# Flamingo block on one core: second normalisation through logarithm and exponential, rows on GpSimd, first shared products between the last projections

## The reference, cut to what matters

```python
def _layernorm(x, eps=1e-05):
    return (x - mean(x)) / sqrt(var(x) + eps)

x = x + tanh(g_xattn) * (softmax(q @ k.T * 16**-0.5) @ v @ W_proj + b_proj)   # q from _layernorm(x), k and v from ctx
n = _layernorm(x)                                # the second normalisation
topw, topi = softmax/top_k(n @ gate_w.T, 2)      # the router
shared = silu(n @ sg_gate.T) * (n @ sg_up.T) @ sg_down.T
x = x + tanh(g_ffn) * (shared + sum over the 2 chosen experts e of w_e * (silu(n @ wg[e].T) * (n @ wu[e].T)) @ w_down[e].T)
```

## Time and profile before

| | us |
|---|---|
| median of 3 runs | 488.83 (488.44 to 489.25) |
| the profiled execution, device time | 488.55 |
| its span in the trace | 486.5 |
| outside the span | 2.05 |
| PE busy | 474.4 (98% of the span) |
| DVE busy | 305.7 (63%) |
| ACT busy | 260.9 (54%) |
| POOL busy | 183.9 (38%) |

### The profile page before, as it was taken

The page is one execution under the profiler, slowest core; times in us unless marked ns, Lnnn a source line. Parts: engine busy times, 40 slices in busy tenths (PEclk is TensorE's granted clock), DMA queues, the critical chain, the costliest instruction groups (busy, mean ns, idle before and its releaser), DMA issues.

```text
span 486.5 us, 7717 instructions
## 1 busy us (share of the span) xinstructions
PE 474.4 (98%) x2765; PEld 283.5 (58%) x2765; DVE 305.7 (63%) x575; ACT 260.9 (54%) x416; POOL 183.9 (38%) x216
## 2 busy tenths in 40 slices
PE   8999999999999999999989999999999999999995
PEld 6655523332333233324445465689799899799994
DVE  3776779999999999997465689632333333323332
ACT  2675277777777777776644501305445346344440
POOL 2830178872321111111000014513556747758433
PEclk9999999999999999999999999999999999999998
DMA  8733408766763555211105001323334533544324
GB/s 245 245 99 103 141 10 241 221 173 192 199 163 80 161 167 165 66 35 55 34 0 174 0 3 43 97 77 77 55 49 65 84 53 68 75 68 67 44 32 44
DMA packets 36789, 48.30 MB, mean 99 GB/s; under 512 B 6288, under 2 KB 29968, under 8 KB 36752
## 3 DMA queue, kind: packets, MB, share of 16 engines
q1 hardware_dynamic: 22112, 26.43, 19.5%
q0 software_dynamic: 7344, 9.84, 13.1%
q10 hardware_dynamic: 7296, 11.54, 7.4%
HBM read 30.16 MB, written 14.29 MB: 91 GB/s over the span
## 4 chain that ended last, share of the span: by engine, by line
PE 88%; DVE 5%; ACT 3%; DMA 2%; issue 1%; POOL 0%; SPq 0%; POOLq 0%
PE ps L1290 69%; PE ps L1382 13%; PE ps L1663 2%; PE ps L1674 2%; DMA wkv_sb<-in_w_kv 2%; DVE neg_max L935 1%; PE ps L1696 1%; ACT up_region L694 1%; ACT rows L688 1%; DVE dn_region L929 1%; DVE rows L900 1%; ACT ctx_region L768 1%; PE ps L1374 0%; PE ps L1535 0%; PE ps L1544 0%
## 5 line engine op out<-in xcount | busy, mean ns | idle before, releaser
L768 ACT ACTIVATE ctx_region<-ps 128x512 f32<-128x512 f32 x256 | 140.7, 594 | 46.9 <-PE ps L1290 46.9
L935 DVE TENSOR_REDUCE neg_max<-ps 128x2 f32<-128x1024 f32 x128 | 150.8, 1209 | 20.9 <-PE ps L1290 18.9
L1290 PE MATMUL ps<-unit_region 96*128 96x512 bf16 (+1 forms) x512 | 128.3, 380 | 1.2 <-ACT ctx_region L768 0.7
L1290 PEld LDWEIGHTS ps<-unit_region 96*128 96x128 bf16 (+1 forms) x512 | 45.0, 97 | 101.3 <-ACT ctx_region L768 45.2
L1290 PE MATMUL ps<-unit_region,ctx_region 128*128 128x128 f32 (+1 forms) x824 | 97.4, 274 | 0.0
L1290 PEld LDWEIGHTS ps<-unit_region,ctx_region 128*128 128x128 f32 (+1 forms) x824 | 94.3, 188 | 0.7 <-DVE x_sb L1077 0.3
L662 POOL DMA_INDIRECT out<-unit_region x39 | 61.2, 1570 | 54.2 <-DMA out<-unit_region 32.3
L1290 PE MATMUL ps<-dn_region,unit_region 128*128 (+1 forms) x294 | 70.0, 381 | 0.0
L849 ACT COPY ctx_region<-up_region 128x1536 f32 x33 | 48.5, 1472 | 34.9 <-PE ps L1290 26.3
L1247 DVE TENSOR_TENSOR unit_region<-unit_region,ps 128x384 f32<-128x384 f32 x35 | 19.4, 555 | 71.2 <-ACT unit_region L866 60.5
L1290 PEld LDWEIGHTS ps<-dn_region,unit_region 128*128 128x128 f32 x294 | 53.2, 190 | 8.4 <-issue 2.8
(11 more groups left out here) (201 smaller groups left out, 459.4 us busy)
## 6 DMA issues: line engine op xcount, KB each, us to landing
up_region<-in_w_upT ACTq DMA_DIRECT2D x9, 768.0 KB, 4.7
qk_parts<-up_region SPq DMA_DIRECT2D x24, 192.0 KB, 3.0
unit_region<-qk_parts SPq DMA_DIRECT2D x24, 192.0 KB, 3.9
dn_region<-in_w_downT ACTq DMA_DIRECT2D x9, 384.0 KB, 5.3
unit_region<-up_region SPq DMA_DIRECT2D x48, 64.0 KB, 2.6
unit_region<-qk_parts SPq DMA_DIRECT2D x24, 128.0 KB, 4.0
x_rows<-rows SPq DMA_DIRECT2D x4, 512.0 KB, 3.3
out<-x_sb SPq DMA_DIRECT2D x4, 512.0 KB
```

Source lines behind the costliest of these rows:

```text
L768: nc.scalar.activation(probs[:, k % 8, :], bank(SCORE_HOME[u, k]), ACT.Exp).then_inc(exp_done, 1)
L935: nc.vector.tensor_reduce(neg_max[:, s, 2 * p:2 * p + 2], bank(2 * (p % 2), 2), AX.X, ALU.max, negate=True).then_inc(max_done, 1)
L1290: return nc.tensor.matmul(o_, w, m, start=start, stop=stop)
```

## The change

ACT now makes 1/sqrt(variance + eps) itself as exp(-0.5 * ln(variance + eps)), from one table set that also holds the Exp of the scores and is loaded once, after the Tanh. For batches 0 and 1 this happens inside the last unit, after the Exps of steps 1 and 11. POOL makes the normalised rows of batches 0 to 2; DVE keeps batch 3. PE turns the rows of batch 0 after step 7 of the last unit, DVE copies them to SBUF, and the four products of the shared expert's chunk 0 go between the last projections. PE's order behind them is new: `turn_rows(1)`, `turn_rows(2)`, `shared_up(0, 1)`, `turn_rows(3)`, `shared_up(0, 2)` with all `router` calls between its halves, and `turn_logits` last. Some PSUM banks change: batch 0 is turned into banks 0 and 1, batches 1 to 3 all into banks 6 and 7. SP stores the rows of a batch when POOL (or DVE) has made them.

```diff
+TURN_FIRST_ROWS = 7
+RSTD_AT = (1, 11)
...
-            return bank(2 + t % 2 if t < NT - TB else (0, 3, 1, 2)[t % TB])[:, 0:D]
+            return bank(2 + t % 2 if t < NT - TB else (4, 5, 1, 2)[t % TB])[:, 0:D]
...
-            return bank(((4, 5), (6, 7), (6, 7), (2, 5))[b][c])
+            return bank((0 if b == 0 else 6) + c)
...
+            for b in range(B - 1):
+                pool.wait_ge(rstd2_done, b + 1)
+                for t in range(b * TB, (b + 1) * TB):
+                    last = nc.gpsimd.tensor_scalar(rows[:, t, :], x_sb[:, t, :], mean_var[:, t, 0:1], rstd[:, t:t + 1],
+                                                   ALU.subtract, ALU.mult)
+                last.then_inc(early_rows, 1)
...
             nc.scalar.activation(tanh_g[:, :], gates[:, :], ACT.Tanh).then_inc(tanh_done, 1)
+            nc.scalar.preload_act_table_set("natural_log_exp_and_others")
...
+                    if u == UNITS - 1 and k in RSTD_AT:
+                        rstd_of(RSTD_AT.index(k))
+
+            def rstd_of(b):
+                act.wait_ge(var_done, B + b + 1)
+                nc.scalar.activation(std[:, b * TB:(b + 1) * TB], mean_var[:, b * TB:(b + 1) * TB, 1], ACT.Ln,
+                                     bias=eps_sb[:, 0:1]).then_inc(log_done, 1)
+                act.wait_ge(log_done, b + 1)
+                nc.scalar.activation(rstd[:, b * TB:(b + 1) * TB], std[:, b * TB:(b + 1) * TB], ACT.Exp, scale=-0.5
+                                     ).then_inc(rstd2_done, 1)
...
-            for b in range(B - 1):
-                std_of(b, B + b + 1)
-
+            rstd_of(2)
...
-            copy_rowsT(0)
             copy_rowsT(1)
-            std_of(3, B + 4)
             copy_rowsT(2)
+            rstd_of(3)
             copy_rowsT(3)
...
+                    if t == NT - TB - 3:
+                        dve.wait_ge(rowsT_ps, B + 1)
+                        for c in range(DC):
+                            last = nc.vector.tensor_copy(xnT[:, c, 0:T], rowsT_bank(0, c))
+                        last.then_inc(first_rowsT, 1)
...
-            ln_apply(0, B + 1)
-            ln_apply(1, B + 2)
...
             stats2(3)
-            ln_apply(2, B + 3)
-            ln_apply(3, B + 4)
+            dve.wait_ge(rstd2_done, B)
+            ln_rows(range(NT - TB, NT)).then_inc(rows_done, 1)
...
+            def turn_rows(b):
+                if b < B - 1:
+                    pe.wait_ge(early_rows, b + 1)
+                else:
+                    pe.wait_ge(rows_done, B + 1)
+                if b >= 2:
+                    pe.wait_ge(rowsT_sb, B + b - 1)
...
+            def first_shared(half, c):
+                col = half * HALF
+                last = mm(bank(3 * half), w_up[:, E, c, col:col + P], xnT[:, c, 0:T], c == 0, c == DC - 1)
+                if (half, c) == (1, DC - 1):
+                    last.then_inc(sh_up_ps, 1)
...
+                if (i, k) == (1, TURN_FIRST_ROWS):
+                    turn_rows(0)
...
             pe.wait_ge(attn_done, B * DC - 1)
+            pe.wait_ge(first_rowsT, 1)
             project_half(NT - 2, 0)
+            pe.wait_ge(w_ffn_in, 16 * 2 * (E + 1))
+            first_shared(0, 0)
             pv(UNITS - 1, (UNITS - 1) % NG, TB - 1)
             pe.wait_ge(x1_done, NT - TB)
             for t in (NT - TB, NT - TB + 1, NT - 1):
                 project_half(t, 0)
+            first_shared(0, 1)
             for q in range(2):
                 pe.wait_ge(attn_done, B * DC + q)
                 for t in range(NT - TB + 2 * q, NT - TB + 2 * q + 2):
                     project_half(t, 1)
+                first_shared(1, q)
...
-                pe.wait_ge(rowsT_sb, B + max(b, 2) + 1)
+                if b == 0:
+                    pe.wait_ge(rowsT_sb, B + 3)
...
-            turn_rows(0)
             turn_rows(1)
-            pe.wait_ge(w_ffn_in, 16 * 2 * (E + 1))
-            pe.wait_ge(rowsT_sb, B + 1)
-            pe.wait_ge(x1_done, NT - 2)
-            shared_up(0, 0, True)
             turn_rows(2)
-
-            def turn_last_rows():
-                turn_rows(3)
+            pe.wait_ge(x1_done, NT)
+            shared_up(0, 1, True)
+            turn_rows(3)
+
+            def route_all():
                 for b in range(B):
                     router(b)
-            pe.wait_ge(rowsT_sb, B + 2)
-            pe.wait_ge(x1_done, NT)
-            shared_up(0, 1, True, between=turn_last_rows)
+            shared_up(0, 2, True, between=route_all)
             turn_logits()
-            shared_up(0, 2, True)
```

More of the change, by code:

```diff
@@ L341, in build @@
         std_done = sem("std_done")
+        log_done, rstd2_done = sem("log_done"), sem("rstd2_done")
+        early_rows, first_rowsT = sem("early_rows"), sem("first_rowsT")
         rstd_done = sem("rstd_done")
@@ L501, in _ @@
             for b in range(B):
-                sp.wait_ge(rows_done, B + b + 1)
+                if b < B - 1:
+                    sp.wait_ge(early_rows, b + 1)
+                else:
+                    sp.wait_ge(rows_done, B + 1)
                 sp.dma_start(x_rows_by_tile[:, b * TB:(b + 1) * TB, :], rows[:, b * TB:(b + 1) * TB, :]).then_inc(rows_out, 16)
@@ L1499, in _ @@
             pe.wait_ge(small_in, 16 * 3)
+            def turn_rows(b):
+                if b < B - 1:
+                    pe.wait_ge(early_rows, b + 1)
+                else:
+                    pe.wait_ge(rows_done, B + 1)
+                if b >= 2:
+                    pe.wait_ge(rowsT_sb, B + b - 1)
+                for t in range(TB):
+                    for c in range(DC):
+                        last = nc.tensor.transpose(rowsT_bank(b, c)[:, t * P:(t + 1) * P],
+                                                   rows[:, b * TB + t, c * P:(c + 1) * P], ident[:, :])
+                last.then_inc(rowsT_ps, 1)
+            def first_shared(half, c):
[3 more added lines that the diff above has]
+                    last.then_inc(sh_up_ps, 1)
             def project_between(i, k):
@@ L1525, in _ @@
                     project_half(t, 1)
-            def turn_rows(b):
-                pe.wait_ge(rows_done, B + b + 1)
-                if b == 2:
-                    pe.wait_ge(rowsT_sb, B + 2)
-                elif b == 3:
-                    pe.wait_ge(x1_done, NT)
[L1533 to L1537, removed]
+                first_shared(1, q)
             def router(b):
-                pe.wait_ge(rowsT_sb, B + max(b, 2) + 1)
+                if b == 0:
+                    pe.wait_ge(rowsT_sb, B + 3)
                 for c in range(DC):
```

## The result

The changed kernel takes 491.67 us (median of 9 runs, 489.59 to 492.43) against 488.71 (9 runs): ratio 1.0048, 95% interval 1.0036 to 1.0061: slower. By the medians it is 3.0 us; the ratio is closer to that of the means (491.14 against 488.73), which lie 2.4 us apart. The two differ because the nine runs fall into two groups. Four lie at 489.59 to 490.43 with a mean granted clock of 0.999 to 1.0, five at 491.67 to 492.43 with 0.995 or 0.996. The median is the lowest run of the second group: with one run more in the first it would have been 490.43. The profiled execution (492.14, span 490.0) belongs to the second group.

A forecast was written before the change was run, and what follows sets the result against it. PE was taken as the bound, busy throughout 272.2 to 470 us. It is free 1.92 us earlier but waits 2.7 us for DVE's chunk, starting 0.79 later: 488.83 + 0.8 = 489.6 us, range 488.8 to 492.2.

The forecast's parts named there:

- The stall: PE before the shared expert's second batch: idle 2.7 us for DVE's first hidden chunk behind the logits; start 0.79 us later.
- The forecast: Whole kernel: 489.6 us, with the second batch 0.79 us late and the clock holding; chance 0.60.
- rival (a): PE's stall before the second batch drops its clock, costing 2.1 us more: 491.7 us; chance 0.28.
- a fallen clock: Sign against the prediction: PE's clock falls in the idle of 2.6 us behind `turn_logits`.
- The price: Cost of a fallen clock: 18 small matmuls at cold start took 4.2 us against 2.1, so 2.1 lost.
- the bound of 0.2%: About 0.2% (0.98 us) of the kernel's time is what a measurement can tell from no change.
- Part 1: Last attention unit: early transposes 0.93 us, Ln and Exp 0.53, POOL's row operation 0.73; last `pv` starts 250.22 against 249.12.
- Part 2: PE's tail from the last `pv`: 1.3 us idle before `turn_rows(2)`, batch 3 ready 0.3 us early, `turn_logits` done at 270.21.
- Part 3: Tables and queues: the prologue's new table load (1.28 us) costs nothing under ACT's idle; earlier row stores precede gathers by 50 us.
- Rival (b): ACT's Ln and Exp each force a table load, 2 x 1.28 us a pair: 494.3 us; chance 0.05.
- Rival (c): The first hidden chunk does not hold PE up at the second batch, keeping 1.92 us: 486.9 us; chance 0.07.

The follow-up runs named there:

- Experiment 1: Changed kernel with Silus and products of hidden chunks 0 and 1 moved ahead of the logits on ACT and DVE: 487.48 us, ratio 0.9971.
- experiment 3: Kernel before, with only PE's new order: whole third chunk of batch 0, router between its halves, ahead of turning the logits: 492.32 us, ratio 1.0079.
- experiment 2: Changed kernel with 16 filler transposes of the identity on PE behind `turn_logits`, results unused: 490.45 us, ratio 1.0039.
- experiment 6: Changed kernel with DVE's 16 MAX8 done twice more ahead of the first hidden chunk, lengthening PE's stall: 494.97 us, ratio 1.0121.
- experiment 5: Changed kernel with batch 3's rows turned between the second chunk's halves and logits between the third's, after the router: 490.01 us, ratio 1.0019.
- experiment 7: Experiment 1 with batch 2 turned into banks 2 and 5, so PE need not wait for ACT's copy of batch 1: 485.99 us, ratio 0.994.
- 9: Changed kernel with 21 filler transposes of the identity on PE behind `turn_logits`, results unused: 490.5 us, ratio 1.0028.
- experiment 4: Kernel before, with only the logarithm and exponential table set load added behind the Tanh: 488.78 us, ratio 0.9999.
- experiment 10: Experiment 1 with the early products undone: batch 0 turned behind the last projections, its four products in one piece: 488.51 us, ratio 0.9985.

## Why the prediction was right, and where not

**The stall.** Right in place, cause and size. Forecast: `turn_logits` issued 19.99 us after the last `pv` starts, chunk 2.7 us later, second batch 0.79 us late. Measured: 271.00 + 0.44 - 251.28 = 20.16, then 2.71, and the second batch 1.00 late, counted from the start of the last unit. Experiment 1 shows the cause by taking it away, experiment 3 by adding it alone.

**The clock.** This is the step that decided, and I weighted it too low. The forecast (489.6, 0.60) was that the clock holds; rival (a) (491.7, 0.28) that it falls. The prediction gave a fallen clock as a sign that it is wrong, and in the profiled execution it fell. Four of nine runs did the one (their mean is 490.1), five the other (492.0), and the median fell into the second group, at 491.67, where (a) had put it. That it matches (a) to 0.03 us is luck. The price was 2.1 in the forecast, 1.5 us in the trace and 1.9 between the means of the groups, and its source is weak: the 18 small matmuls at the kernel's start, which took 4.2 us, took 3.61 in the changed kernel's trace (1.5 us by the same working), and the profile gives both stretches a granted clock of 1.00, so it does not show that the clock made them slow.

The chance had been read from one fall at the kernel's end, 2.24 us after the last matmul. That row was enough to name the case and too little to weigh it. In the twelve traces the fall at that place comes anywhere from 2.3 to 5.1 us after the last matmul: 2.3 in three of them (the kernel before, experiments 2 and 6), 4.9 or more in four (3, 5, 7 and 9). In the stall of the changed kernel it came after 2.0. A stall of 2.55 us lies at the short end of this spread, so it could go either way, and one of 1.30 lies below all of it. The page's rule (the Trainium skill, TensorE: Matmul & The Clock Gate, "What's actually happening") says that the chip looks at TensorE's activity in windows that run freely, not aligned with the kernel; the two outcomes at one idle length (a fall in the changed kernel's trace, none in experiment 3's) and the spread at the kernel's end agree with that. What I had drawn from it, that a stall shorter than a window never costs anything and the time is 489.6, is not what the stall of 2.55 us did in five of nine runs.

**My direction.** Slower had 0.55 and same 0.36; it was slower, clear of the bound of 0.2%. The single number I gave was on the edge of "same", 2.1 us under the result; the range up to 492.2 held it, because it took in rival (a). Even the group whose clock held lies 0.5 us over the forecast; the changed stretch accounts for 0.2 of that (1.00 in place of 0.79), and the rest is open.

**Part 1.** The last unit went as written: 0.93 us forecast for the eight transposes, 0.88 measured (243.03 to 243.91), Ln and Exp 0.52 against 0.53, the last `pv` 1.14 us later relative to the unit's start (251.28 - 235.16 against 249.12 - 234.14). DVE's two copies took 1.29, inside 0.8 to 1.7. POOL's row operation was mis-sized: 0.73 taken, 1.22 measured, inside the bounds. It cost nothing, since batch 0 was ready at 242.54 and needed at 243.03, but the cover (the time by which the rows were early) shrank from 2.5 us to 0.5. Batch 2's rows were there at 258.58, 1.7 us before use; in experiment 7 only 0.3 are left.

**Part 2.** The idle of 1.3 us ahead of `turn_rows(2)`: 1.25. The rows of batch 3: ready at 264.30, transposes at 264.61, so 0.3 us ahead as forecast.

**Part 3.** The table load cost nothing (experiment 4). The earlier stores of the rows were not tried by themselves; the kernel behind the changed stretch took as long as before. Rival (b) fell: no load at either pair. Rival (c) fell: PE did wait.

**What the change is worth without the stall:** 1.3 us (experiment 1), not the 1.92 that rival (c) would have kept; 0.7 to 1.0 of it is the early turning and the products laid between the projections (experiment 10).

## What to carry to other kernels

A step moved to the end of one engine's stretch also moves everything that stands behind its result in another engine's list: here two independent pieces of work (a hidden chunk, the routing) shared DVE's list in the wrong order, and putting the one that PE needs first turned a loss of 3 us into a gain of 1.3 (3.0 with experiment 7's banks). A stall of TensorE can have a second price beyond its length: here the one of 2.55 us had it in some executions, the one of 4.99 us in all four, and those of 1.30 us and less in none as far as the clocks show. Break it up, fill it, or move the wait, and look at every run's time and at the clock of the stretch in a trace, rather than at the median alone. Before copying such an edit, see whether the engine it loads has idle time there: the same edit in the old order cost 1 us.

## What the runs showed of the hardware that I had not expected

With TensorE idle, the granted clock fell 2.0 us after the last matmul in the changed kernel, 3.8 in experiment 6, and 2.3 to 5.1 at the end of the twelve profiled kernels; in experiment 3's trace it did not fall in 2.55 us at all. In the traces with waits of 0.83 and 1.30 us (experiment 5) and 0.80 (experiment 2) it held, and none of the ten other runs of experiment 5 is above 490.4. With 4.99 us it fell in all 4 runs, by the trace of one and the means of the rest. Once down it stayed for 3.4 us in the changed kernel and for 6.8 in experiment 6.

GpSimd's tensor_scalar with two per-partition operands took 1.22 us for 128x256 floats, where its tensor_tensor of that size took 0.73 and VectorE's tensor_scalar a quarter of 1.38.
